# ViT tower with a two-expert MLP on one core: dump rows written block by block, and another order of the mixer's pieces

## What is computed

```python
h = tok(x)                                  # 16 images x 256 tokens x 256 features
h = concat([cls_tok, h], axis=1)            # 257 rows per image
h = h + attn(layernorm(h))                  # gated linear recurrence along the tokens
h = h + ffn(layernorm(h))

# tok:  y = sigmoid(q) * (ew @ (ek*v)) / (ew @ ek);  layernorm(y @ out_w + out_b + x)
# attn: r,i = sigmoid(x@W_r), sigmoid(x@W_i); a_t = a*r
#       h_t = a_t*h_{t-1} + (1-a_t)*i*(x@W_in);  h @ W_out
# ffn:  shared MLP(256-1024-256, gelu) + the best 2 of 8 experts of the same size,
#       each weighted by the softmax of its router logit
```

## Time and profile before

| | us |
|---|---|
| median of 3 runs | 982.86 |
| the profiled execution | 984.09 |
| its span, first to last instruction | 982.0 |
| steps 0 to 3 | 0 to 116.7 |
| steps 4 to 13 | 116.7 to 406.7 |
| steps 14 to 18 and the class row's product | 406.7 to 525.6 |
| change of stage, PE nearly idle | 525.6 to 536.6 |
| experts | 536.6 to 972.1 |
| end | 972.1 to 982.0 |

### The profile page before, as it was taken

How to read it: one execution, slowest core, us unless ns; L and a number is a source line. 1 busy time by engine, 2 the same in 40 slices (tenths; PEclk the granted TensorE clock), 3 DMA queues, 4 the chain that set the end, 5 groups by cost and what they waited for, 6 DMA issues and landing times.

```text
span 982.0 us, 21456 instructions
## 1 busy us (share of the span) xinstructions
PE 921.2 (94%) x6825; PEld 858.8 (87%) x6825; DVE 700.6 (71%) x2093; ACT 482.3 (49%) x1146; POOL 394.2 (40%) x475
## 2 busy tenths in 40 slices
PE   7887999999999999999995999999999999999995
PEld 5665988888888888887985999999999999999995
DVE  3578788999999999999886464645646565654643
ACT  2123455555455555454341555555555555555553
POOL 6442233444333444315553334343533434342322
PEclk9898899999999999999997999999999999999998
DMA  9600001111101111101662728282642827473222
GB/s 257 187 22 23 30 31 50 54 54 54 46 18 43 54 54 54 54 1 40 199 220 69 220 44 220 43 221 43 161 107 44 219 44 190 77 205 60 44 43 33
DMA packets 50536, 89.11 MB, mean 91 GB/s; under 512 B 6733, under 2 KB 31199, under 8 KB 50498
## 3 DMA queue, kind: packets, MB, share of 16 engines
q0 software_dynamic: 31440, 58.52, 24.8%
q1 hardware_dynamic: 19058, 30.11, 10.8%
HBM read 59.28 MB, written 29.09 MB: 90 GB/s over the span
## 4 chain that ended last, share of the span: by engine, by line
PE 36%; DVE 27%; issue 23%; POOL 9%; ACT 3%; POOLq 1%; DVEq 1%; DMA 0%; ACTq 0%; SPq 0%
PE ps_nd L810 11%; PE ps_proj L794 5%; POOL out L755 5%; DVE rden L1996 4%; PE ps_ri L794 3%; DVE GL L1810 3%; PE ps_ip L960 3%; PE ps_ip L794 3%; PE ps_h L975 3%; DVE w2l L2228 2%; DVE st L1827 2%; PE ps_proj L889 1%; PE ps_proj L891 1%; PE ps_proj L894 1%; DVE h L1833 1%
## 5 line engine op out<-in xcount | busy, mean ns | idle before, releaser
L1810 DVE TENSOR_TENSOR GL<-g_act,GH 128x256 fp32r<-128x256 f32 (+1 forms) x416 | 174.6, 426 | 168.1 <-ACT GH L1440 152.9
L810 PE MATMUL ps_nd<-w2h,GH 128*128 128x256 f32 x832 | 242.5, 291 | 6.1 <-DVE Y L1999 4.8
L1435 ACT ACTIVATE g_act<-ps_proj,fcb 128x256 f32<-128x256 f32 (+1 forms) x272 | 129.1, 475 | 234.9 <-PE ps_proj L794 226.3
L810 PE MATMUL ps_nd<-w2h,GL 128*128 128x256 f32 x832 | 234.2, 281 | 0.0
L810 PE MATMUL ps_nd<-w2l,GH 128*128 128x256 f32 x832 | 233.3, 280 | 0.0
L810 PEld LDWEIGHTS ps_nd<-w2h,GH 128*128 128x128 f32 x832 | 156.6, 188 | 12.2 <-DVE Y L1999 5.0
L1440 ACT CAST GH<-g_act 128x256 fp32r<-128x256 f32 (+1 forms) x416 | 161.3, 400 | 1.2
L810 PEld LDWEIGHTS ps_nd<-w2l,GH 128*128 128x128 f32 x832 | 157.4, 189 | 0.0
L810 PEld LDWEIGHTS ps_nd<-w2h,GL 128*128 128x128 f32 x832 | 156.7, 188 | 0.0
L794 PE MATMUL ps_proj<-xh,w1h 128*128 128x256 f32 (+1 forms) x544 | 122.6, 307 | 12.6 <-DVE E L1989 8.9
L755 POOL DMA_INDIRECT out<-yb,rows_to x72 | 115.5, 1605 | 16.8 <-issue 13.2
(11 more groups left out here) (281 smaller groups left out, 1932.1 us busy)
## 6 DMA issues: line engine op xcount, KB each, us to landing
R<-v_rows SPq DMA_DIRECT2D x37, 260.0 KB
w1h<-fc_w POOLq DMA_DIRECT2D x9, 1024.0 KB
w2h<-pj_w POOLq DMA_DIRECT2D x9, 1024.0 KB
stage<-fc_w POOLq DMA_DIRECT2D x9, 1024.0 KB
stage<-pj_w POOLq DMA_DIRECT2D x9, 1024.0 KB
x<-x SPq DMA_DIRECT2D x28, 256.0 KB, 4.0
v_rows<-tail_rows SPq DMA_DIRECT2D x8, 520.0 KB
out<-yb SPq DMA_DIRECT2D x16, 256.0 KB
```

The costliest lines, as they stand in the source:

```text
L810: last = pe.matmul(banks[a], g[:, j, a * P:(a + 1) * P], w[i][:, j, :], start=(j == 0 and q == 0), stop=(j == HT - 1 and q == 2))
L1435: act.activation(g_act[:, j % G_SLOTS, 0:width], banks[j % len(banks)][:, 0:width], ACT.Gelu_apprx_tanh, bias=fcb[i][:, j:j + 1]).then_inc ...
L1810: dve.tensor_tensor(GL[:, j, 0:width], g_act[:, j % G_SLOTS, 0:width], GH[:, j, 0:width].bitcast(F32), ALU.subtract).then_inc(gl_done, 1)
```

## The change

1. `seconds`, `tails` and `ends_i` go. A new `fill(t)` on SP, one per step, writes dump rows into block `t` of all eight lists: 2048 rows of 1040 bytes, 2.13 MB, for `t` = 0 to 16. It waits until all earlier fills have landed. `rows_out` of image `n` waits for `n+2` fills, `cls_out` for one.
2. The block limits are computed inside the mixer's last step: `block_bounds` right behind `slots_out(18)`, `block_places` before the last `base_sum`.
3. In the experts' stage DVE adds and multiplies one half and then the other, and POOL waits for each half by itself.
4. SP copies the class row when the blocks before the last have been added, and POOL waits for the last addition.
5. The order of pieces changes in all three parts on PE, ACT and DVE, and in the written-out parts on POOL. POOL's `step` is unchanged.

```diff
@@ SP
+            def fill(t, par):
+                if isinstance(t, int) and t == 0:
+                    sp.wait_ge(lines, 2)
+                after(sp, filled, 16 * t)
+                sp.dma_start(v_rows[0:DUMP, :].rearrange("(e l) m -> e l m", e=NE)
+                             [:, bass.ds(t * BLK, BLK), :].rearrange("e (p a) m -> p e a m", a=2),
+                             tail_rows[:].unsqueeze(1).to_broadcast([P, NE, 2, W])
+                             ).then_inc(filled, 16)
             def step(t, par):
                 x_in(t, par)
+                fill(t, par)
                 base_out(t, par)
             x_in(2, 0)
-            seconds(2, 0)
             x_in(3, 1)
+            fill(0, 0)
+            fill(1, 1)
+            fill(2, 0)
+            fill(3, 1)
...
-            tails(18, 0)
...
-            sp.wait_ge(added, end * 32 + 32)
-            sp.wait_ge(rows_loaded, end * 16 + 16)
+            sp.wait_ge(added, end * 32)
@@ POOL
-                    if isinstance(n, int) and n == 0:
-                        pool.wait_ge(seconds_stored, 16 * NE)
-                    if isinstance(n, int) and n == NIMG - 1:
-                        pool.wait_ge(tails_stored, 16 * NE)
+                    pool.wait_ge(filled, 16 * (n + 2))
...
+            low_second(2, 0)
             rstd_h(2, 0)
             affine(2, 0)
             rstd_u(2, 0)
             out_bias(2, 0)
-            low_second(2, 0)
...
-                pool_wait(pool, y_done, b * 2 + (2 * SBLK + 2), "y").then_inc(carried, 1)
                 for a in range(2):
+                    pool.wait_ge(carried, b * 3 + (a + 2))
+                    pool_wait(pool, y_done, b * 2 + (2 * SBLK + a + 1), "y").then_inc(carried, 1)
@@ PE, step
                 hidden(t, par, 4)
+                rank(t, par)
                 turn_u(t, par)
                 hidden(t, par, 5)
                 hidden(t, par, 6)
-                rank(t, par)
+                hidden(t, par, 7)
                 gates0(t, par)
+                turn_v(t, par)
                 input0(t, par)
-                turn_v(t, par)
                 gates1(t, par)
                 ffn_out(t, par, 0)
-                input1(t, par)
...
-                hidden(t, par, 7)
...
                 ffn_out(t, par, 7)
+                input1(t, par)
@@ ACT, step
+                x_high(t, par)
                 gelu_j(t, par, 1)
                 high(t, par, 1)
-                x_high(t, par)
@@ DVE, step
                 u_stats(t, par)
+                low(t, par, 0)
                 second(t, par)
                 u_norm(t, par)
...
                 low(t, par, 4)
+                low(t, par, 5)
+                v_low(t, par)
                 gate_a(t, par)
                 y_last(t, par)
-                low(t, par, 5)
-                slots_out(t, par)
                 low(t, par, 6)
                 low(t, par, 7)
-                v_low(t, par)
                 x_low(t, par)
+                slots_out(t, par)
                 gate_b(t, par)
                 base_sum(t, par)
@@ DVE, last steps
+            places(18, 0)
             low(18, 0, 0)
...
+            slots_out(18, 0)
+            block_bounds(18, 0)
...
+            block_places(18, 0)
             base_sum(18, 0)
```

More of the change, by code:

```diff
@@ L2445, in mixer_vector @@
+            h_norm(17, 1)
+            v_norm(16, 0)
+            u_stats(17, 1)
             low(16, 0, 3)
-            second(16, 0)
             ratio1(17, 1)
-            v_norm(16, 0)
-            ekv0(17, 1)
+            places(16, 0)
+            u_norm(17, 1)
             low(16, 0, 4)
+            v_low(16, 0)
+            slots_out(16, 0)
+            low(16, 0, 5)
             gate_a(16, 0)
-            h_norm(17, 1)
-            low(16, 0, 5)
-            places(16, 0)
             low(16, 0, 6)
-            u_stats(17, 1)
@@ L2502, in mixer_vector @@
             low(18, 0, 3)
-            v_sum(18, 0)
             low(18, 0, 4)
+            low(18, 0, 5)
+            ratio1(18, 0)
             u_norm(18, 0)
-            low(18, 0, 5)
             low(18, 0, 6)
+            u_low(17, 1)
+            u_low(18, 0)
+            x_low(15, 1)
             low(18, 0, 7)
-            u_low(18, 0)
-            v_norm(18, 0)
+            block_places(18, 0)
             base_sum(18, 0)
-            v_low(18, 0)
+            y_last(18, 0)
+            ekv1(18, 0)
@@ L2538, in experts_vector @@
-            dve.tensor_scalar(cnt["skip"][:], cnt["blocks"][:], -1.0, float(LIST_BLKS),
-                              ALU.mult, ALU.add)
-            dve.tensor_copy(hop[:, NE - 1, :], block_f[:])
-            chain(dve.memset(carrier["count"][:], 0.0))
-            for e in range(NE - 1):
-                last = dve.tensor_scalar(hop[:, e, :], block_f[:], cnt["end"][:, e:e + 1],
-                                         cnt["skip"][:, e:e + 1], ALU.is_ge, ALU.mult)
-            chain(last)
-            chain(dve.tensor_reduce(where[:], hop[:].rearrange("p e b -> p b e"), AX.X, ALU.add))
```

661 lines of the change are left out of this document (325 added, 336 removed).

## The result

The changed kernel takes 1001.7 us in the median of 4 runs (1000.1 to 1003.5), the kernel before 982.9 us (982.4 to 986.0). The ratio is 1.0189, with a 95% interval of 1.0168 to 1.0209. The change makes the kernel 1.9% slower. The forecast was 977.0 us, in a range of 965 to 990, so it had the wrong sign.

| stretch, bounds on PE | before | after | difference | forecast |
|---|---|---|---|---|
| steps 0 to 3 | 116.7 | 116.6 | -0.1 | -3.3 |
| steps 4 to 13, the loop | 289.9 | 295.2 | +5.3 | +5.4 |
| steps 14 to 18 with the class row's product | 118.95 | 138.1 | +19.1 | -0.2 |
| change of stage, to the first block's first product | 10.95 | 2.35 | -8.6 | -5.0 |
| experts, to PE's last product | 435.5 | 439.0 | +3.5 | -0.5 |

The account below looks back on a forecast made before the run. The loop was taken as a circle through DVE, PE nearly full, with POOL's circle binding after the change. Terms -3.3 + 5.4 - 1.5 - 3.7 - 0.5 - 2.4 = -6.0 gave 977.0 us beside 982.86, range 965 to 990.

Parts of the forecast that it names:

- Steps 14 to 18: Last mixer steps: new lists may close or reopen PE's 7 us of gaps, work unchanged; -1.5 us (+3 to -5).
- +1.3 for the limits: Last MLP of step 18: places, slots_out and block_bounds stand between low parts 0 and 1, ending it 1.3 us later.
- The loop: Steps 4 to 13: slots_out behind x_low makes POOL's circle the bound, 29.53 us a step instead of 28.99; +5.4 us.
- the first rival: Loop: POOL's circle does not bind, 28.6 us a step, -4.1 instead of +5.4, 967.5 us in all; chance 0.20.
- the second: Loop: scatters stay long, POOL part 9.1 instead of 7.85 us, slower than before at 990 us; chance 0.17.
- Steps 0 to 3: First steps: DVE is the bound and the new list brings h_sum(3) earlier; -3.3 us (+2 to -6).
- The third rival: Steps 0 to 3 and 14 to 18: the new lists bring nothing, 4.8 us gone, 982 us; chance 0.18.
- The fills: SP's dump-row writes, 17 times 2.13 MB, 8 us each until landed: nothing on the path in the loop.
- The sign that I had named for being wrong here: Fills: the prediction is wrong there if ACT waits for x.
- Change of stage: Mixer to experts: early limits let PE start its block 5.9 instead of 10.95 us after the class row's product; -5.0 us.
- Clock and experts: After the change of stage: a shorter gap saves some lower-clock time, -0.5 us (0 to -1.6); the halves cost nothing that shows.
- End: After PE's last product: SP's copy runs beside the last block, the span ends with the last addition's landing; -2.4 us.

Follow-up runs that it names:

- e4: Changed kernel, POOL only: rows_out of step 16 ahead of weight 1's loads, weight 1's four low-half subtractions behind the start of the experts; 1006.0 us, ratio 1.0210.
- e8: Changed kernel with POOL's four subtractions for weight 1's low halves given to DVE as eight pieces; 990.3 us, ratio 1.0071.
- e9: Changed kernel with only weight 1's loads moved in POOL's list, from ahead of rows_out of step 16 to ahead of rstd_h of step 16; 994.0 us, ratio 1.0092.
- e5: Changed kernel with two things taken back: DVE makes both yt halves, waits once, then both yb halves; the last wait is DVE's; 996.1 us, ratio 1.0130.
- b5: Changed kernel's lists with slots_out ahead of x_low, weight 1's loads earlier, low halves on DVE, old yb order, DVE's last wait, places behind xl; 979.3 us, ratio 0.9952.
- e7: Changed kernel with one line moved in DVE's loop step: slots_out back ahead of x_low; 993.5 us, ratio 1.0087.
- e6: Kernel before with one line moved in DVE's loop step: slots_out behind x_low; 997.9 us, ratio 1.0146.
- e1: Kernel before with the changed kernel's lists of one loop step on PE, ACT and DVE, nothing else; 988.4 us, ratio 1.0043.
- b1: Kernel before's lists, with the fills, limits behind the last low part, old order of yb's halves and last wait on DVE; 980.7 us, ratio 0.9976.
- e3: Changed kernel with the old lists of steps 14 to 18 on PE, ACT, DVE and POOL, limits right behind slots_out(18); 994.5 us, ratio 1.0103.
- b2: As b1, with weight 1's low halves on DVE in eight pieces and the blocks' places behind xl of block 0; 975.9 us, ratio 0.9928.
- b3: As b2, with the changed kernel's lists in steps 0 to 3 and the loop, slots_out ahead of x_low; 974.2 us, ratio 0.9915.
- b6: As b3, with the blocks' places ahead of xl, and spare PE products of zeros, three ahead of block 0's transposes and six behind; 973.4 us, ratio 0.9889.
- e2: Kernel before with the changed kernel's lists of steps 14 to 18 on all engines, tails and late limits kept; 997.0 us, ratio 1.0130.

## Why the prediction was wrong

**Steps 14 to 18 (-1.5, +1.3 for the limits, measured +19.1).** This is the step that failed. It said that the lists "may close in part or open again; the work is unchanged", and took a small number without walking them, though all four engines had new lists there. Two facts were at hand. The earlier trace rows shows a DVE sum at 3.80 us beside POOL's subtractions, and I used it for `pack_split` in step 2, but never asked which DVE operation the same POOL pieces would meet in steps 17 and 18. And the diff puts `rows_out(16)` behind the loads, while `v_norm(17)` waits for its scatters: the very kind of queue that a moved step has to be walked past. Shown: the pairs (e4, e8), the queue (e9 against e5, some 2 us), the lower clock behind the gaps, and 3 us from the new order of PE and DVE itself (e4, b5).

**The rule that I cited and used in one place only.** The Trainium skill (SBUF — State Buffer, "Who interferes with whom") has GpSimd and a VectorE operation with two SBUF inputs exclude each other for a whole instruction, when the GpSimd operation reads SBUF. The traces agree: POOL's small operation held up beside `x_low` in e7 (1.77 us), the two-input operations caught in steps 14 to 18, and the sums with an operand in PSUM that were not (0.79 us for two). That DVE was out there for both of POOL's back-to-back instructions (4.63 us for two of 2.3) goes beyond the rule. It is not always so: in e4's first steps DVE got in between the two (2.25 us, and then caught again).

For the scatters the page does not carry what I took from it. Of DMA descriptors it speaks for VectorE's two-port mode, and it says that `tensor_tensor`, which `x_low` is, was not seen to stall a DMA. The rows decide: ten scatters of 2.07 us and more that start during `x_low` in the kernel before, none over 1.19 us in the changed kernel, where none does.

**The loop (+5.4, measured +5.3).** Right, mechanism and size: POOL's part 7.99 us for 7.85, DVE's 21.5 for 21.68. Some of the precision is luck. I took DVE's part as the same in any order; in e6, where only this line is moved, it is 22.46 us and the loop costs 13 us more, so without the other moved pieces the same sum would have been 8 us short. Neither the first rival (POOL's circle doesn't bind) nor the second (scatters stay long) came.

**Steps 0 to 3 (-3.3, measured -0.1).** The third rival's case. `h_sum(3)` came at 90.13 us, not at 86.4. `pack_split` lost 2.8 us beside POOL's halves as forecast (3.97 for 1.2), but not into slack: `turn_y(2)` on PE waits for Y behind it.
```profile
49.81 3.97 DVE L2223 TENSOR_TENSOR w2h<-wproj,w2h 65x1024 fp32r<-65x1024 f32 x1
56.51 1.11 PE L891 MATMUL ps_t<-ident,Y 128*128 128x128 f32 x4 [4.14 <-DVE Y L2078]
90.13 0.69 DVE L1999 TENSOR_TENSOR h<-xr,ps_h 128x512 f32<-128x512 f32 x1 [0.20 <-PE ps_h L965]
```
From `turn_y(1)` to `turn_y(4)` the six kernels with the old lists take 84.9 to 87.1 us, the twelve with the new ones 84.4 to 87.4. The two orders are worth the same; that `pack_split` ate the gain is argued, not tested alone.

**The fills (nothing on the path).** Right. One lands in 9.0 us in the median (8 forecast), and they cost 0.7 us in the loop (e1 against the changed kernel). The sign that I had named for being wrong here did come: ACT waits for x, 9.9 us in nine places. But e1, without fills, has 9.0 us in nine places; so it comes with the new order of the loop, and the fills add 0.9.

**Change of stage (-5.0, measured -8.6).** Better than forecast: the transposes follow the class row's product at once, at 549.77, so the register loads, which I charged at 3.5 us, were over by then. The limits were ready at 535.75, and I read it so that PE's sequencer went through the loads while PE still waited and multiplied; no run separates that. In b1, whose limits came at 526.6, the transposes came 3.75 us later. Of the early limits it is true that they pay only if they meet no pair and stand behind the low parts (e3, b1, b2).

**Clock and experts (-0.5, measured +3.5).** The clock gave nothing back: it was 0.50 again behind the shorter gap, and the first block takes 10.9 us up to the next transposes in both kernels. I costed the halves of yb at nothing because DVE is half idle. DVE is not the point, its turn is: a wait between the halves makes the next low parts late (e5, 3.3 us).

**End (-2.4, measured +0.6).** I took the landing of the last addition for the end of the span. The mis-sized term is what passes after it: 3.7 us with POOL last, 2.2 with DVE last.

## What to carry to other kernels

When a list of pieces is reordered, walk every stretch of it, the short lists at the edges too, and for each long operation of one engine ask what the other engine will have in hand just then; a piece that is hidden today is hidden by where it stands. Ask it of the right ones: in these traces a PSUM operand saved an operation from POOL's pairs, and two SBUF inputs exposed it, however small it was. An operation that can shut out another engine for 5 us belongs on that engine itself (the same subtractions cost DVE 5.0 us of its own, in eight pieces, and 11.7 us are won), or behind a wait of the engine that it would catch. A one-line move can turn a slack circle into the bound: add up the chain behind a piece through every engine before moving it.

## What the runs showed of the hardware

- In steps 14 to 18 a pair of POOL subtractions of 1024 columns each (2.35 us) keeps a DVE operation out for the whole pair: 0.17 to 0.18 us became 5.00 (comparison, 128x16) and 5.31 (conversion, 128x8). In both records the caught operation starts ahead of POOL's pair, by 0.32 and 0.55 us, and its duration grows; it is not shown as a wait. In e4's first steps DVE came in between the two (2.25 us for a copy of two columns).
- Not caught by the same pairs: sums with an operand in PSUM (two in 0.79 us, e5).
- The other way round, beside a DVE operation of 2.00 us with two SBUF inputs a POOL operation on one element took 1.77 us (e7), and a scatter 2.07 to 2.10 instead of 1.04 (before).
- Behind the gaps of 5.15 and 3.10 us the granted clock was 0.50 (for instance from 526 to 528 and from 546 to 548); in steps 14 to 18 there are 12.7 us more of gaps and 6.5 us more of PE's busy time. Behind gaps of 1.28 and 1.73 us in b3 it fell as well; with spare products in them it stayed at 1.00 (b6). Behind gaps of nearly the same length, 1.28 and 1.68 us in e8 and 1.58 and 1.56 in b5, it stayed at 1.00 without any, so the length of the gaps alone does not tell.
- Where 4 MB of loads stood right ahead of the scatters on POOL's queue, `v_norm` waited 2.2 to 3.3 us for them to land (after, e2, e5, e7, e8); with the loads some 30 us earlier it waited 0.3 us, for POOL and not for a landing (e9).
- Where the end of the program lies depends on the engine that ends last (3.7 us, 2.2 us).
- The first 30 us vary: the same code reaches the same point at 28.5 us in one kernel's profiled execution and at 37.1 in another's.
